# A four-layer graph network on one core: two message steps joined to the end of a convolution, one reduction in place of two additions, dense weights loaded earlier

## The reference, cut to what matters

```python
x = x + L0(h)   # relational convolution: 8 bases of 512x512, edge coefficients, segment sum by dst
x = x + L1(h)   # two graph convolutions, 512 -> 512 -> 512, with self-loops
x = x + L2(h)   # message layer, below
x = x + L3(h)   # two dense aggregations (agg @ W_l.T + x @ W_r.T + b), tanh between them
```

```python
hs = xs @ w_in2f_s / sqrt(128);  hv = einsum('nbc,bf->nfc', xv, w_in2f_v) / sqrt(128)
s, v = hs[idx_j], hv[idx_j]                     # 32 scalars and 3 x 32 vector parts of each edge
t_s2 = einsum('efc,ec->ef', v, yv) / sqrt(3)    # the dot product over the three directions
Wf   = ((ssp(f_ij @ W1 + b1) @ W2 + b2) * rcut_ij[:, None]).reshape(-1, 32, 6)
edge = [s*ys*Wf0, t_s2*Wf1, s*yv*Wf2, v*ys*Wf3, ...]     # only the first four feed the output
agg  = segment_sum(edge, idx_i)                 # then two small dense products
```

## Time and profile before

| what | value |
|---|---|
| median of three runs | 1456.11 us |
| the profiled execution | 1456.16 us |
| its span | 1454.3 us, so 1.86 us lie around the span |
| PE busy | 1364.6 us, 94% |
| POOL busy | 892.1 us, 61% |
| DVE busy | 861.3 us, 59% |
| ACT busy | 494.5 us, 34% |
| message stage, first POOL gather to last PE accumulation | 856.4 to 1185.2 us |
| after the message stage | 1185 to 1454 us, POOL idle |

### The profile page before, as it was taken

The page is one execution under the profiler, slowest core; times in us unless marked ns, Lnnn a source line. Parts: engine busy times, 40 slices in busy tenths (PEclk is TensorE's granted clock), DMA queues, the critical chain, the costliest instruction groups (busy, mean ns, idle before and its releaser), DMA issues. The chain is left out here.

```text
span 1454.3 us, 24122 instructions
## 1 busy us (share of the span) xinstructions
PE 1364.6 (94%) x6924; PEld 937.1 (64%) x6925; DVE 861.3 (59%) x2485; ACT 494.5 (34%) x1279; POOL 892.1 (61%) x927
## 2 busy tenths in 40 slices
PE   4888799999999999999999989998999979999998
PEld 2778788888885444444694866665666656686565
DVE  8778755555554667776433429988888854411111
ACT  7000000000005888882521235654555546311100
POOL 5777777777777777777777767777777720000000
PEclk9999999999999999999999989999999989999999
DMA  4678789888885652233211122222222330000000
GB/s 164 193 228 232 237 288 312 259 239 257 269 263 159 171 163 83 76 84 110 57 26 26 37 60 59 71 65 64 74 67 65 87 77 1 30 0 30 8 29 35
DMA packets 104166, 172.96 MB, mean 119 GB/s; under 512 B 20155, under 2 KB 54128, under 8 KB 104080
## 3 DMA queue, kind: packets, MB, share of 16 engines
q0 software_dynamic: 42832, 103.15, 24.2%
q10 hardware_dynamic: 27790, 39.30, 8.8%
q1 hardware_dynamic: 33458, 29.39, 6.5%
HBM read 153.74 MB, written 18.02 MB: 118 GB/s over the span
## 5 line engine op out<-in xcount | busy, mean ns | idle before, releaser
L874 POOL DMA_INDIRECT gath<-h_rows,idx x313 | 303.0, 968 | 95.0 <-issue 66.8
L1008 PEld LDWEIGHTS ps<-spread,gath 128*128 128x128 f32 x2504 | 306.9, 197 | 73.8 <-issue 43.4
L1008 PE MATMUL ps<-spread,gath 128*128 128x96 f32 x2504 | 313.0, 281 | 24.6 <-DMA gath<-h_rows,idx 17.7
L1030 PE MATMUL ps<-base_t,z 128*128 128x512 f32 (+1 forms) x640 | 308.4, 603 | 0.0
L930 POOL DMA_INDIRECT u<-u_rows,at x219 | 218.6, 998 | 66.8 <-issue 63.4
L1550 DVE TENSOR_TENSOR z<-z,ps 128x384 f32 x313 | 172.7, 552 | 100.1 <-PE ps L1008 88.5
L900 POOL DMA_INDIRECT slots<-att,idx_s x160 | 161.6, 1010 | 49.5 <-issue 47.6
L1221 PE MATMUL ps<-msg,hot 128*128 128x256 f32 x648 | 162.4, 394 | 20.6 <-DVE msg L1922 19.5
L900 POOL DMA_INDIRECT slots<-z,idx_s x153 | 153.5, 1003 | 43.9 <-issue 41.2
L1221 PEld LDWEIGHTS ps<-msg,hot 128*128 128x128 f32 x648 | 119.2, 192 | 81.0 <-DVE msg L1922 59.8
L1030 PEld LDWEIGHTS ps<-base_t,z 128*128 128x128 f32 (+1 forms) x640 | 107.3, 188 | 75.1 <-issue 74.9
(11 more groups left out here) (297 smaller groups left out, 1837.8 us busy)
## 6 DMA issues: line engine op xcount, KB each, us to landing
base_t<-in_bases_dram ACTq DMA_DIRECT2D x116, 256.0 KB
slots<-att SPq DMA_DIRECT2D x21, 256.0 KB, 5.2
at<-slots SPq DMA_DIRECT2D x21, 256.0 KB, 2.7
gath<-h_rows,idx POOLq DMA_INDIRECT x313, 4.2
u<-u_rows,at POOLq DMA_INDIRECT x219, 2.5
att<-in_attr_dram SPq DMA_DIRECT2D x40, 64.0 KB
slots<-att,idx_s POOLq DMA_INDIRECT x160
z<-in_attr_dram SPq DMA_DIRECT2D x39, 64.0 KB
```

The lines of the kernel that those rows point to most:

```text
L874: nc.gpsimd.indirect_dma_start(out=gath[:, c % RING, :], out_offset=None, in_=h_rows, in_offset=bass.IndirectOffsetOnAxis(ap=idx[:, par, c ...
L1008: last = mm(bank[:, k * SPREAD:(k + 1) * SPREAD], gath[:, h_slot, k * P:(k + 1) * P], s_of.rearrange("p b d -> p (b d)"), start=True, stop ...
L1030: return mm(ps[BANKS[n]][0:rows(n), :], z[:, k, b, n * P:n * P + rows(n)], base_t[:, k, :], start=(t == JOINS[n]), stop=(t == JOINS[n] + T ...
```

## The change

Three edits. SP loads the dense weights after the quads 0 to 7 (four pairs) in place of after all 21. PE and ACT take the steps -4 and -3 into the last two turns of the convolution's loop: `at_step(-4)` ahead of `u_product(9)` and its evacuation, `at_step(-3)` behind them. DVE sums the dot product with one `tensor_reduce` over three values, and `v_ok` counts three in a step.

```diff
-            steps(sp, RADIALS // 2, 1, 0, sorted_pair, skip=1)
+            MIDDLE = 4
+            steps(sp, MIDDLE, 1, 0, sorted_pair, skip=1)
+            sp.wait_ge(out_ok, AGG[2])
+            sp.wait_ge(m_ok, RING)
+            for t, w in ((wa, s_w1l), (wb, s_w1r)):
+                sp.dma_start(t[:, :, :], w.rearrange("(k p) f -> p k f", p=P)).then_inc(ld_w3, 16)
+            sp.dma_start(b_a[:, 0:KIN], s_b1).then_inc(ld_w3, 16)
+            sp.dma_start(b_b[:, :], s_b2.to_broadcast([P, FEAT])).then_inc(ld_w3, 16)
+
+            steps(sp, RADIALS // 2, MIDDLE, 0, sorted_pair, skip=MIDDLE)
             sorted_quad(RADIALS - 1, 0)
             sp.wait_ge(u_ev, BLOCKS)
...
-
-            sp.wait_ge(out_ok, AGG[2])
-            sp.wait_ge(m_ok, RING)
-            for t, w in ((wa, s_w1l), (wb, s_w1r)):
-                sp.dma_start(t[:, :, :], w.rearrange("(k p) f -> p k f", p=P)).then_inc(ld_w3, 16)
-            sp.dma_start(b_a[:, 0:KIN], s_b1).then_inc(ld_w3, 16)
-            sp.dma_start(b_b[:, :], s_b2.to_broadcast([P, FEAT])).then_inc(ld_w3, 16)
...
@@ ACT, behind the evacuation of u_product(n - 2) in the loop over n
-            radial(*at_step(-4))
-            act.wait_ge(ld_mp, 16 * 13)
-            radial(*at_step(-3))
+                if n == BLOCKS:
+                    radial(*at_step(-4))
+                if n == BLOCKS + 1:
+                    act.wait_ge(ld_mp, 16 * 13)
+                    radial(*at_step(-3))
             radial(*at_step(-2))
...
@@ PE, behind u_product(n - 2) in the loop over n
-                message(*at_step(-4))
-                pe.wait_ge(ld_mp, 16 * 13)
-                message(*at_step(-3))
+                    if n == BLOCKS:
+                        message(*at_step(-4))
+                    if n == BLOCKS + 1:
+                        pe.wait_ge(ld_mp, 16 * 13)
+                        message(*at_step(-3))
                 message(*at_step(-2))
...
@@ DVE, one step
-                    dve.wait_ge(v_ok, st * 4 + 1)
-                    v.tensor_tensor(v_sum[:, :, :], vy[:, :, 0, :], vy[:, :, 1, :], ALU.add).then_inc(v_ok, 1)
+                    dve.wait_ge(v_ok, st * 3 + 1)
+                    v.tensor_reduce(v_sum[:, :, :], vy[:, :, :, :].rearrange("p c y f -> p c f y"), mybir.AxisListType.X, ALU.add)\
+                        .then_inc(v_ok, 1)
                     dve.wait_ge(p_ok, st + 1)
                     v.tensor_tensor(out_v[:, :, :, HID:2 * HID],
                                     py[:, par, :, HID:2 * HID].unsqueeze(2).broadcast_to([P, QUAD, 3, HID]), uv, ALU.mult)
-                    dve.wait_ge(v_ok, st * 4 + 2)
-                    v.tensor_tensor(v_sum[:, :, :], v_sum[:, :, :], vy[:, :, 2, :], ALU.add).then_inc(v_ok, 1)
                     v.tensor_tensor(sw[:, :, :], w[:, :, 3 * HID:P], us, ALU.mult).then_inc(v_ok, 1)
                     v.tensor_tensor(msg[:, par, :, 0:HID], py[:, par, :, 0:HID], us, ALU.mult)
-                    dve.wait_ge(v_ok, st * 4 + 3)
+                    dve.wait_ge(v_ok, st * 3 + 2)
                     v.tensor_tensor(msg[:, par, :, HID:2 * HID], w[:, :, 2 * HID:3 * HID], v_sum[:, :, :], ALU.mult)
-                    dve.wait_ge(v_ok, st * 4 + 4)
+                    dve.wait_ge(v_ok, st * 3 + 3)
                     v.tensor_tensor(out_v[:, :, :, 0:HID], sw[:, :, :].unsqueeze(2).broadcast_to([P, QUAD, 3, HID]), y,
                                     ALU.mult).then_inc(m_ok, 1)
```

## The result

The changed kernel takes **1463.53 us** (median of four runs, 1463.09 to 1466.76) where the kernel before takes 1455.73 us (four runs): ratio **1.0063**, 95% interval 1.0049 to 1.0077. It is 0.6% slower; 1451.5 us was forecast. The profiled executions are 1463.09 us with a span of 1461.3 us, and 1456.16 us with a span of 1454.3 us, so 7.0 us are to be found.

A forecast was written before the change was run, and what follows sets the result against it. The prediction took POOL's gathers, three a step, to bound the message stage. From the profiled 1456.16 us: - 3.26 (early load) + 0.07 (reduction) - 1.5 (POOL) = 1451.5 us, range 1448.0 to 1456.5 us.

The forecast's parts named there:

- The early load, -3.26 us: Message stage's end: without the weights' load, step 80's gap falls to 1.65 us and DVE starts it 3.26 us earlier.
- rival (b): At the stage's end: the weights did not make the gather late, so the 4.03 us stay; 1454.7 us, chance 0.11.
- In its new place 0: Moved load near step 24: DVE stalls about 4 us but POOL issues on; cost 0, bounds 0 and 1.4 us.
- Rival (a): Message stage after 960 us: DVE runs free, four gathers lengthen, POOL loses 3.9 us; 1456.9 us, chance 0.15.
- POOL -1.5 us: POOL's gathers: the reduction breaks DVE's train, so POOL's path shortens 1.5 us; bounds 5 us less, 3 us more.
- the forecast of 0.85 us each: Six long gathers: with the train broken behind `hot`, POOL could enter 0.85 us earlier each time, 5.1 us in all.
- The bound of 3 us: POOL's path: the worst case allowed, 3 us more, for shifted phases, new meetings and a second free-running stretch.
- Reduction on DVE's path, +0.07 us: DVE's step 80: a reduction of 0.47 us replaces two operations' 0.40 us, adding 0.07 us to the path.
- rival (c): DVE in the message stage: a reduction of 0.94 us makes DVE the bound; 1473 us, chance 0.06.
- The joined steps, 0: Before the message stage: DVE's step 0 comes 0.8 to 1.0 us earlier, worth 0 at the end; bounds 0 and 1.1 us.

The follow-up runs named there:

- h_joined_load_spread: The kernel before plus joined steps, early load and padding slots naming 128 different rows, with the two sums kept: 1455.29 us, ratio 0.9998.
- h_after: The whole change run again on another chip, against the kernel before at 1455.22 us: 1466.54 us, ratio 1.0069.
- g_no_reduce: The whole change without the reduction (early load and joined steps only), against the kernel before at 1455.01 us: 1456.65 us, ratio 1.001.
- g_spread: The kernel before with padding slots naming 128 different rows instead of all row 0: 1454.18 us against 1455.01 us, ratio 0.9989.
- e1_early_load: The kernel before with the early weight load alone, on a chip that takes about 2050 us: ratio 0.999 (0.9953 to 1.0026).

## Why the prediction was wrong
- **"The early load, -3.26 us": the step that failed.** It took the gap of 4.91 us at step 80 for the weights' doing, because the stall of 4.03 us at step 77 was theirs. The stall was (it is gone in every kernel with the early load), but the last six gathers' 128 reads of one row would have held step 80 at nearly the same time: 4.62 us remained. This is rival (b)'s outcome for the end, by another mechanism. The sign was in reach: DMA share and GB/s at 1172 to 1178 us in the kernel before, behind the weights, were not looked at for the gathers alone. They are 0.76 at 53 GB/s, then 0.53 and 0.66 at 33 GB/s: busy engines that move little. With spread rows the tail does shrink by what was forecast, 12.2 to 8.9 us, 3.3 us; the run time still falls by only 1.6 us between the medians, not parted from zero, since the next term takes its share.
- **"In its new place 0."** DVE did stall 3.78 us at step 24 and was back on POOL at step 32, and POOL's wait at `at_free` did not come, as the text had it. But the free-running stretch cost POOL 2.4 to 4.0 us in gathers 72 to 100 against 0.4 to 1.2. Rival (a) had named this, at 3.9 us. PE's clock fell behind the moved stall too (granted clock 0.50 from 968 to 970 us), without effect, since POOL paces there.
- **"POOL -1.5 us": sign wrong**, +3.4 us in the profiled execution and +9 to +11 us in the two later ones of the same message stage. What the text said of the mechanism held: the train is broken, and none of the gathers of over 1.5 us begins 0.45 us behind `hot` any more, where four did. A gather that begins just ahead of a step's `vy`, with no pause in DVE's work, takes 2.12 us (887.96 us) where it took 2.99 us, so the forecast of 0.85 us each was right. (The prediction's 907.49 us for L1917 should read 907.53; such gathers end 0.90 to 0.91 us behind the start that frees them, not 0.95, which changes the sum by nothing that counts.) Not weighed was that the third product moves from 1.27 to 1.58 us behind `vy`, onto the very place where a delayed gather's follower begins. The bound of 3 us was "phases shift", with no phase worked out.
- **Reduction on DVE's path, +0.07 us.** It measured 0.50 us to the next start (0.58 us long) where 0.47 was taken: +0.1 us, right in size. DVE did not become the bound; rival (c) did not occur.
- **The joined steps, 0.** Step 0 came 3.2 us earlier (870.26 against 873.50 us), not 0.8 to 1.0, and no gather moved for it. One pair of executions doesn't size this: from the first gather to step 0 it is 13.6 to 16.6 us in the six kernels with joined steps and 15.0 to 18.8 us in the four without. `h_joined_load_spread` shows no cost. Right in what it is worth.
- **Not foreseen:** PE's clock. Two late steps in a row left PE idle for 1.46 and 3.33 us, the granted clock fell to 0.50, and 2.8 us were lost in the last sums and closing rows. In `h_after` the sums again took 3.59 us; with spread rows, 1.99 us. In `g_no_reduce`, with idle times of 1.24 and 2.97 us in the same two steps, the clock stayed at 1.00 and the sums at 1.99 us. So this part of the loss shows only with load and reduction together.

How the loss divides is shown in time on the chip of the last runs at 1455 us: of 11.3 us, 6.6 leave with the spread rows (tail and clock) and 4.6 with the reduction, which on the other chip costs 4.4 us by itself. Early load, joined steps and spread rows together then take the time before: by the tables the end gains 3.2 us and the gathers lose it. That the first chip's 7.8 us divide alike is likely, not shown. The forecast came to -4.7 us because it counted a gain at the end that the padding rows withheld and gave POOL a gain where meetings made a loss.

## What to carry to other kernels
When a transfer is taken off a stall, ask what else would be late at that moment, and look at share and GB/s together: full engines at 50 GB/s are not the same cause as full engines at 370 GB/s. When two engines share a resource in a rhythm, an edit of 0.1 us to one can lock it onto the other's followers; write down where in the step each wide operation begins, before and after, beside the interval of the disturbed partner. Give padding entries of an indirect gather different rows where they are the last thing waited for; alone, in `g_spread`, it gained nothing that shows.

## What the runs showed that was not expected
- A gather that begins 0.05 to 0.43 us behind the start of `vy` ends 0.90 us behind the next operation's start, 1.35 to 1.39 us behind `vy` (18 of 19); begun earlier than 0.05 us it was undisturbed (7 of 7), and so were 44 of 44 behind the single-input reduction.
- Indirect gathers whose 128 indices name one row land so late that DVE starts 3.6 to 4.6 us behind the issue's end (four kernels with the early load); with 128 different rows it is 1.6 to 1.7 us (three kernels), with DMA shares of 1.13 and 1.23 against 0.25 and 0.19.
- Chips differ: the same kernel before takes 1455 to 1456 us on three and 2048 to 2066 us on four, with engines at rest for up to 26 us without a cause in the profile (read in `e1_early_load`). There the reduction gained 1.8%, and moving one addition 0.7 to 1.0% (base: 0.3%, not parted from zero). Why is open.
